# Nine small tiles change places in on-chip memory in front of and behind the transposed token rows

## The reference

```python
x = x + xattn(layernorm(x), k_cache=ctx, v_cache=ctx)   # 4096 context rows + 256 new ones, one head of 512
x = x + attn(layernorm(x))                              # 16 heads, low-rank q and kv, rotary part of 64, causal
x = x + ffn(layernorm(x))                               # 32 routed experts (8 per token) + a shared one
# ffn, routed:  silu(x @ w_gate[e]) * (x @ w_up[e]) @ w_down[e], weighted by the router
```

## Time and profile before

| | |
|---|---|
| median of 3 runs | 530.5 us |
| profiled execution | 531.82 us |
| its span, first to last instruction | 529.8 us |
| matmuls, weight loads | 3454 each |
| PE busy | 518.0 us, 98% of the span |
| VectorE, ScalarE busy | 388.9 us, 304.2 us |
| granted TensorE clock | 1.00, mean of the span |

### The profile page before, as it was taken

How to read it: one execution, slowest core, us unless ns; L and a number is a source line. 1 busy time by engine, 2 the same in 40 slices (tenths; PEclk the granted TensorE clock), 3 DMA queues, 4 the chain that set the end, 5 groups by cost and what they waited for, 6 DMA issues and landing times.

```text
span 529.8 us, 9657 instructions
## 1 busy us (share of the span) xinstructions
PE 518.0 (98%) x3454; PEld 464.5 (88%) x3454; DVE 388.9 (73%) x616; ACT 304.2 (57%) x470; POOL 29.4 (6%) x48
## 2 busy tenths in 40 slices
PE   9999999999999999989999999999999999999997
PEld 7878888888678988869999999999999999999997
DVE  6677655557888987877896767777686777768675
ACT  5656486655367775655654564646655465555631
POOL 1000000000623122001000000000000000000000
PEclk9999999999999999999999999999999999999999
DMA  8765534554512242424536455564645546464521
GB/s 287 288 214 183 195 123 126 172 171 141 150 35 77 75 145 94 129 111 173 186 123 229 151 210 183 173 206 157 230 151 206 186 171 213 151 230 155 201 71 40
DMA packets 19459, 86.24 MB, mean 163 GB/s; under 512 B 2160, under 2 KB 2416, under 8 KB 19312
## 3 DMA queue, kind: packets, MB, share of 16 engines
q1 hardware_dynamic: 19440, 85.99, 48.1%
HBM read 85.46 MB, written 0.52 MB: 162 GB/s over the span
## 4 chain that ended last, share of the span: by engine, by line
PE 79%; DVE 10%; DMA 6%; ACT 2%; issue 2%; SPq 0%; POOL 0%; ACTq 0%; DVEq 0%
PE bank L936 32%; PE bank L429 14%; PE bank L432 13%; PE bank L433 13%; DVE w_lo L282 3%; DMA raw<-w_exp_dram 2%; DMA raw<-ctx_t_dram 2%; DMA raw<-w_mla_dram 2%; DVE scores L1436 1%; ACT w_hi L277 1%; PE bank L573 1%; PE bank L437 1%; DVE xt_lo L330 1%; DVE operands L309 1%; PE bank L438 1%
## 5 line engine op out<-in xcount | busy, mean ns | idle before, releaser
L277 ACT CAST w_hi<-raw 128x768 fp32r<-128x768 f32 (+3 forms) x158 | 158.9, 1040 | 100.6 <-PE bank L936 83.1
L282 DVE TENSOR_TENSOR w_lo<-raw,w_hi 128x1280 fp32r<-128x1280 f32 (+3 forms) x156 | 182.8, 1214 | 17.1 <-ACT w_hi L277 15.1
L429 PE MATMUL bank<-w_hi,operands 128*128 128x512 f32 (+1 forms) x322 | 126.8, 394 | 2.1 <-DVE operands L330 1.0
L432 PE MATMUL bank<-w_lo,operands 128*128 128x512 f32 (+1 forms) x322 | 123.9, 385 | 0.0
L433 PE MATMUL bank<-w_hi,operands 128*128 128x512 f32 (+1 forms) x322 | 123.8, 385 | 0.0
L936 PE MATMUL bank<-xt_hi,w_lo 128*128 128x256 f32 x512 | 106.9, 280 | 0.0
L936 PE MATMUL bank<-xt_lo,w_hi 128*128 128x256 f32 x512 | 106.9, 279 | 0.0
L936 PE MATMUL bank<-xt_hi,w_hi 128*128 128x256 f32 x512 | 106.8, 280 | 0.0
L936 PEld LDWEIGHTS bank<-xt_hi,w_hi 128*128 128x128 f32 x512 | 82.6, 187 | 2.6
L936 PEld LDWEIGHTS bank<-xt_lo,w_hi 128*128 128x128 f32 x512 | 80.4, 188 | 0.0
L936 PEld LDWEIGHTS bank<-xt_hi,w_lo 128*128 128x128 f32 x512 | 80.4, 188 | 0.0
(11 more groups left out here) (182 smaller groups left out, 564.9 us busy)
## 6 DMA issues: line engine op xcount, KB each, us to landing
raw<-w_exp_dram SPq DMA_DIRECT2D x34, 896.0 KB, 4.8
raw<-w_exp_dram SPq DMA_DIRECT2D x34, 640.0 KB, 5.7
raw<-ctx_t_dram SPq DMA_DIRECT2D x16, 512.0 KB, 4.9
raw<-ctx_n_dram SPq DMA_DIRECT2D x16, 512.0 KB, 4.0
raw<-w_mla_dram SPq DMA_DIRECT2D x8, 512.0 KB, 3.6
raw<-w_mla_dram SPq DMA_DIRECT2D x8, 448.0 KB, 4.0
raw<-wq_dram SPq DMA_DIRECT2D x4, 256.0 KB, 5.4
raw<-wk_dram SPq DMA_DIRECT2D x2, 512.0 KB, 7.2
```

The lines of the kernel that those rows point to most:

```text
L277: act.copy(w_hi[:, t.slot, at:at + n], raw[:, t.slot, at:at + n]).then_inc(hi_split[k], 1)
L282: eng.tensor_tensor(w_lo[:, t.slot, at:at + n], raw[:, t.slot, at:at + n], w_hi[:, t.slot, at:at + n].bitcast(F32), ALU.subtract) \
L429: ins = pe.matmul(o, a[0], b[0], start=start, stop=False)
L432: pe.matmul(o, a[0], b[1], start=False, stop=False)
```

## The change

Six small tiles (`var_eps`, `power`, `rstd`, 24 bytes each; `neg_max`, `exp_bias`, 8 bytes each; `weights`, 272 bytes; rounded up, 448 bytes together) are allocated in front of `xt_hi` instead of behind `mean_var`. Two tiles of 8 bytes (`q_neg`, `q_root`; 64 bytes rounded up) go from in front of `xt_hi` to behind `rope_w`. Shapes, instructions and semaphores are the same. The order of the instructions on every engine is the same, row for row.

```diff
         xn = sb("xn", [P, 2, D])
-        q_neg = sb("q_neg", [P, 2])
-        q_root = sb("q_root", [P, 2])
+        var_eps = sb("var_eps", [P, 6])
+        power = sb("power", [P, 6])
+        rstd = sb("rstd", [P, 6])
+        neg_max = sb("neg_max", [P, 2])
+        exp_bias = sb("exp_bias", [P, 2])
+        weights = sb("weights", [P, 2, NE])
         xt_hi = sb("xt_hi", [P, NC, T], F32R)
         xt_lo = sb("xt_lo", [P, NC, T], F32R)
...
-        var_eps = sb("var_eps", [P, 6])
-        power = sb("power", [P, 6])
-        rstd = sb("rstd", [P, 6])
         row_max = sb("row_max", [P, 2, NG + 1])
-        neg_max = sb("neg_max", [P, 2])
-        exp_bias = sb("exp_bias", [P, 2])
...
-        weights = sb("weights", [P, 2, NE])
         rope_w = sb("rope_w", [P, 2, 4, 512], F32R)
         rope_raw = probs[:, :, :, :].rearrange("p a b n -> p (a b) n")
+        q_neg = sb("q_neg", [P, 2])
+        q_root = sb("q_root", [P, 2])
```

## The result

The changed kernel takes 523.77 us in the median of 20 runs (523.24 to 530.88); the kernel before, in 20 runs, 529.92 us (528.81 to 531.73). That is 6.15 us less; the ratio is 0.9901, with an interval of 0.9884 to 0.9918. One run of the experiments, 568.67 us with xt at 128, had a mean granted clock of 0.85 where all others had 0.999 or 1.00, and is compared with nothing.

A forecast was written before the change was run, and what follows sets the result against it. PE, without a gap from 270 to 523 us, was taken to bound the kernel. Terms -6.0 + 0.1 - 0.1 + 0 = -6.0 us gave 524.5 us (chance 0.43); own range 523.6 to 525.8, 8-in-10 range 523.4 to 532.5.

The forecast's parts named there:

- step 1: gate_up, 30 expert blocks, xt over w: distance +64 to -64, matmul step 117.8 to 113.3 ns; 6.0 us gained.
- 2: Other engines beside a faster PE in the expert blocks: VectorE, ScalarE and DMA keep up, no new wait.
- step 5: 512-column matmuls: values of the new rows, 24 matmuls, 0.1 us gained; down taken as 0, 1.6 us at worst.
- 3: First-stage queries and keys, 96 matmuls: at most 0.43 us shorter, but PE's wait for a split grows equally: 0.
- 4: expert_rows, w over xt, 96 matmuls: distance -64 to +64, up to 0.3 us lost, taken as 0.1.
- 6: Router's weights, rotary weights, transposed tiles, and small VectorE and GpSimd operations at other addresses: taken as 0.
- rival C: Matmul step set by the entry, not the starts, or +64 and -64 are alike: no change, 530.5 us; chance 0.20.
- B: gate_up: only one of two alternating block entries reaches 113.3 ns; 15 blocks gain 3.0 us, 527.5 us; chance 0.16.

The follow-up runs named there:

- the two pads: Kernel before with 384 empty bytes in front of xt_hi and 128 in front of rope_w, no small tile moved: 523.75 us, ratio 0.9898.

## Why the prediction was right

The forecast was 6.0 us less than 530.5, 524.5 us; the time is 523.77, 6.15 less than 529.92. Most of the 0.7 us between forecast and time is the lower median of before. The size came out of small misses that cancel: the blocks gave 5.6 us and not 6.0, `down` 0.3 where nothing was put, and the 0.25 us that are left can't be told from none. By the steps:

1. gate_up was put at 5.7 to 6.4 us, taken as 6.0, with blocks of 5.44 to 5.47. They take 5.47, and 30 x 0.187 = 5.6 us: just under the lower end, as each block does begin with some long steps. The reading by classes, that xt over w at -64 does what operands over w do at -64, held in this loop, and two independent ways of making that distance (xt at 320, w at 0) give the short step again, the second in half the blocks.
2. No new wait: VectorE's busy share of the stretch went from 74% to 76%, and PE has no gap. `down`, put at 0 in step 5, got 0.3 us shorter over the loop.
3. The first stage did get shorter in the trace after (89 steps in 10.09 us, 113.4 ns):

```profile
9.84 0.28 PE L429 MATMUL bank<-xt_hi,w_hi 128*128 128x256 f32 x1
...
19.93 0.28 PE L433 MATMUL bank<-xt_hi,w_lo 128*128 128x256 f32 x1
20.04 0.39 PE L429 MATMUL bank<-w_hi,operands 128*128 128x512 f32 x1
```

   but the wait that was to grow by what PE saves did not come in this trace. The kernel with xt at 448 had the same short stage, waited, and ended at 529.56, no faster than before. The first of the 30 blocks starts between 268.8 and 272.0 us in the traces of the kernels with full loads, with short and long first stages mixed, so 0.4 us more or less ahead of it can't be told from none: 0 is not refuted, and its reason is not shown.
4. `expert_rows` went from 113.3 to 117.8 in the first profile, as said, but stayed at 113.3 in the second profile of the same kernel and with the two pads. The three profiled executions took 523.41, 523.15 and 523.64 us, so it costs nothing that shows.
5. The values of the new rows did not gain their 0.1 us: 512 columns of w over xt take 233.4 ns at +64 as they did at -64. With xt at 320, which is +64 modulo 256 too, they settle at 229 ns (11 steps in 2.52 us, from 70.27 to 72.79). So that class has both steps at +64; the term was too small to matter.
6. The small tiles (eight, six forward and two back, and not nine as the title has it): 0 within the spread, shown by the pads.

The prediction also set a rule of the Trainium skill against its rows, by which no start address could matter and the time would stay at 530.5 us. That did not hold here: empty bytes alone gave 523.75 us. Which part of the rule fails, no run tells.

Two things in the argument were weaker than they looked. The prediction read from its trace that xt over w at +64 settles nowhere but at 117.8; the first stage with xt at 448 held 113.3 at +64, and at -64, with xt at 320, 117.7. And it took the distance as the cause and the entry as the rival C; the runs show that neither alone decides. In gate_up's loop, where the entry repeats, +64 gave 117.8 in three kernels (before, xt at 448, operands at 128) and -64 gave 113.3 in four (the changed kernel, the pads, xt at 320, and every second block with w at 0), but 117.8 in the two where down runs at 226.7 ns. So rivals B and C were real: B is the kernel with w at 0, C the one with xt at 64 and operands at 128, and with another `down` the forecast would have failed by all of step 1. That this `down` leads to the short step was not worked out in the prediction, only given a chance of 0.43; to that extent it was luck.

What stays open: why an entry leads to one step or the other; and the runs near 530 us, 2 of 20 and, with the pads, 1 of 10. Their granted clock is 1.00 as in the others. A loop that holds 117.8 ns all through would be 30 x 0.187 = 5.6 us longer, 529.4 us, which is near but not all of it. `expert_rows` shows that one program can hold either step, but no profile fell on such a run, so it is only argued.

## What to carry to other kernels

Where TensorE has no gap, read the step of its matmuls from the starts in the timeline, by pairs of moving and stationary tile: one shape with several steps in one trace is a sign that the places of the tiles matter, and a few empty bytes in front of one tile then test it. Profile a kernel more than once before a step is put down to its addresses. Change one distance at a time and look at the whole loop: a stretch that gets faster by itself (down at 226.7 ns) can hand over to its neighbour in a way that costs more than it won.

## What the runs showed of the hardware that was not expected

- 256 moving columns with a full weight load beside them, in gate_up's loop, by distance modulo 256 bytes: 0, 120.0 ns; 64, 117.8; 128, 120.0; 192, 113.3, or 117.8 after some entries. Only four places, 64 bytes apart, were tried. Outside the loop, 64 and 192 were each found with both steps.
- One program, unchanged, held 117.8 ns in `expert_rows` in one execution and 113.3 in another.
- 512 columns had their shortest step at another distance: 226.7 ns at 0 in `down`, where 64 had 229 and 192 some 233. For 256 columns 0 was among the worst places.
- 113.3 ns is the shortest step that 256 columns held over 24 matmuls in any of these traces, with a load of 64 columns too; half the load's columns took away what distance 0 costs, and at 64 what every second block has above 113.3.
